# A four-quadrant crossing of query and projection in a window-attention block, and one attention moved at the end

## What is computed

```python
x = x + _conv_bn(x, dw0_w, dw0_s, dw0_b, groups=C)
x = x + _ffn(x, f0_...)
x = x + _windowed_attn(x, wq, wkv, pos, scale_p, dwc_w, dwc_b, proj_w, proj_b)
x = x + _conv_bn(x, dw1_w, dw1_s, dw1_b, groups=C)
x = x + _ffn(x, f1_...)

# _attn, per 7x7 window (the 16x16 image is padded to 21x21, nine windows):
q, kv = xw @ wq.T, xw @ wkv.T              # k gets pos; relu, / softplus(scale)
q, k = _focus(q), _focus(k)                # t**3, norm restored
kv2 = einsum('bjc,bjd->bcd', k, v)         # per head, 4 heads of 16
y = einsum('bic,bcd,bi->bid', q, kv2, z)   # z = 1 / (q . sum k)
y = y + depthwise_5x5(v)
return y @ proj_w.T + proj_b
```

## Time and profile before

| | |
|---|---|
| median of 3 runs | 174.64 us (173.4 to 175.21) |
| the profiled execution | 174.51 us, of which the span from first to last instruction is 172.7 us |
| PE busy | 157.2 us, 91% of the span |
| DVE, ACT, POOL busy | 103.9, 83.7 and 57.5 us (60%, 48%, 33%) |
| mean granted TensorE clock | 0.98 |

### The profile page before, as it was taken

The page is one execution under the profiler, slowest core; times in us unless marked ns, Lnnn a source line. Parts: engine busy times, 40 slices in busy tenths (PEclk is TensorE's granted clock), DMA queues, the critical chain, the costliest instruction groups (busy, mean ns, idle before and its releaser), DMA issues. The chain is left out here.

```text
span 172.7 us, 6668 instructions
## 1 busy us (share of the span) xinstructions
PE 157.2 (91%) x2840; PEld 76.6 (44%) x2840; DVE 103.9 (60%) x270; ACT 83.7 (48%) x178; POOL 57.5 (33%) x75
## 2 busy tenths in 40 slices
PE   6977999899898999999996789999989999987893
PEld 3312252627274873583383562576433425222231
DVE  1168263858777778597588586582189476606043
ACT  2054869494937665756745414653431414033132
POOL 4000028260825504263934926640254312000000
PEclk9999999999999999999999956999999999999999
DMA  5999999940000000000054161063027181959943
GB/s 144 291 245 292 212 215 208 206 84 6 0 4 4 4 4 4 0 4 4 28 141 78 66 143 35 4 171 72 4 76 163 63 173 66 189 167 218 299 140 121
DMA packets 18028, 18.77 MB, mean 109 GB/s; under 512 B 1104, under 2 KB 17744, under 8 KB 17872
## 3 DMA queue, kind: packets, MB, share of 16 engines
q1 hardware_dynamic: 17568, 17.83, 44.6%
q10 hardware_dynamic: 432, 0.52, 1.1%
HBM read 14.16 MB, written 4.19 MB: 106 GB/s over the span
## 5 line engine op out<-in xcount | busy, mean ns | idle before, releaser
L649 PE MATMUL ps<-xc,dwf 96*32 96x480 f32 (+3 forms) x408 | 44.9, 575 | 3.4 <-DMA xc<-mid 2.4
L371 POOL TENSOR_TENSOR qt<-q 128x512 f32<-128x512 f32 x8 | 10.7, 1333 | 57.2 <-ACT q L465 57.2
L649 PEld LDWEIGHTS ps<-xc,dwf 96*32 96x32 f32 x408 | 12.1, 112 | 32.7 <-issue 24.2
L424 ACT ACTIVATE x<-ps,wts 128x512 f32<-128x512 f32 x15 | 10.3, 685 | 26.0 <-PE ps L649 26.0
L671 PE MATMUL ps<-x,w1s 64*128 64x512 f32 x60 | 16.7, 637 | 2.9 <-DVE kvm L1107 1.4
L431 ACT ACTIVATE hid<-ps,wts 128x512 f32<-128x512 f32 x27 | 17.2, 682 | 3.2 <-PE ps L671 3.2
L677 PE MATMUL ps<-hid,w2s 128*64 128x512 f32 x60 | 17.2, 614 | 0.0
L377 POOL TENSOR_TENSOR y<-y,fm 128x512 f32<-128x512 f32 x8 | 10.2, 1274 | 10.7 <-DVE y L1161 7.7
L1061 DVE TENSOR_REDUCE nrm<-k 128x10 f32<-128x640 f32 x8 | 6.6, 819 | 11.6 <-ACT k L459 11.5
L358 POOL TENSOR_TENSOR k<-k 128x640 f32<-128x640 f32 x8 | 12.4, 1550 | 3.4 <-ACT k L453 3.4
L734 PE MATMUL ps<-wts,x 64*64 64x128 f32 x256 | 11.2, 294 | 0.6 <-DVE y L1161 0.6
(11 more groups left out here) (139 smaller groups left out, 277.7 us busy)
## 6 DMA issues: line engine op xcount, KB each, us to landing
xc<-in_x SPq DMA_DIRECT2D x16, 240.0 KB, 11.4
xc<-mid SPq DMA_DIRECT2D x16, 240.0 KB, 4.7
xc<-in_x SPq DMA_DIRECT2D x8, 256.0 KB, 10.7
mid<-x SPq DMA_DIRECT2D x8, 256.0 KB, 2.2
xc<-mid SPq DMA_DIRECT2D x8, 256.0 KB, 3.3
out<-x SPq DMA_DIRECT2D x7, 256.0 KB, 5.7
tab<-in_tables SPq DMA_DIRECT2D x1, 1024.0 KB, 11.4
wts<-in_weights SPq DMA_DIRECT2D x1, 644.0 KB, 7.2
```

The costliest lines, as they stand in the source:

```text
L371: eng.tensor_tensor(qt[:, g % QB, 0:GC], q2[:, g % 2, 0:GC], q1[:, :], ALU.mult).then_inc(qt_ready, 1)
L424: eng.activation(x1[:, m % 2, :], bank(m % 2), ACT.Identity, bias=ww(f"dwb_{m // NG}")).then_inc(x1_ready, 1)
L649: last = eng.matmul(out_ps[32 * q:32 * q + 32, :, :, to], dwf[:, s, q % 2, i, :], src[:, :, :, of], start=(i == 0), stop=False, skip_group ...
```

## The change

Query and projection, which each were two matmuls of 512 columns on the quadrants (0, 0) and (1, 1), become four matmuls of 256 columns on all four quadrants. Image (a, j) of the query goes to column half r = a ^ j and bank `P_B + j`, so q comes out with two of its four images crossed in the partitions; k times v, `window_conv` and the buffers `vfull` and `fm` follow that crossing, and the projection crosses back. With it the banks change: the query fills both banks of `P_B`, the projection of groups 0 to 3 goes to `P_H`, of groups 4 and 5 to a convolution bank and bank 7, of groups 6 and 7 to `P_A`. The waits follow the banks. In slots 6, 7, 9 and 10 `attend` stands ahead of `ffn1`; on DVE `q_first` stands ahead of `k_focus` (slots 5, 6) or ahead of `take_y` (slots 7, 8). At the end `attend(7)` stands directly behind `project(4)`, `conv(11)` behind `project(5)` and `turn_y(6)`, and `project(6)` ahead of `ffn1(11)`; on DVE `take_y(7)` stands ahead of `second(10)`.

```diff
+        def proj_banks(c):
+            if c < 4:
+                return P_H, P_H + 1
+            return (spare(9 + c), P_B + 1) if c < 6 else (P_A, P_A + 1)
...
 def conv(m, n, js=slice(0, GP)):
-                if 0 <= n - 8 < 4:
-                    eng.wait_ge(xw_ready, n - 7)
+                if m in (11, 12):
+                    eng.wait_ge(x3_ready, m - 6)
...
 def ffn1(m, n):
+                if 0 <= n - 7 < 4:
+                    eng.wait_ge(xw_ready, n - 6)
                 if m == 13:
-                    eng.wait_ge(y_ready, NG)
+                    eng.wait_ge(x3_ready, NG)
...
 def query(g, n):
-                for a in range(2):
-                    p = slice(64 * a, 64 * a + 64)
-                    last = eng.matmul(bank(P_B + 1)[p].rearrange("p (j n) -> p j n", j=GP), ww("wq")[p], x2[p, g, :, 0:PX],
-                                      start=True, stop=True)
+                for a, r in QUADRANTS:
+                    j = a ^ r
+                    last = eng.matmul(bank(P_B + j)[64 * r:64 * r + 64, 0:PX], ww("wq")[64 * a:64 * a + 64],
+                                      x2[64 * a:64 * a + 64, g, j, 0:PX], start=True, stop=True)
...
 def kv_rest(g, n):
+                if n == NG:
+                    eng.wait_ge(xw_ready, 2)
...
 def key_value_full(g, n):
-                            last = eng.matmul(bank(P_B + wx)[64 * a:64 * a + 64, VC * s:VC * s + VC], kf[p, g % 2, a, s, :],
-                                              vfull[p, g, 4 * a + s, :], start=True, stop=True)
+                            last = eng.matmul(bank(P_B + wx)[64 * (a ^ j):64 * (a ^ j) + 64, VC * s:VC * s + VC], kf[p, g % 2, a, s, :],
+                                              vfull[p, g // 4, 4 * a + s, g % 4, :], start=True, stop=True)
...
 def turn_y(c, n):
+                if n <= NG:
+                    eng.wait_ge(q_ready, n)
...
 def project(c, n):
                 eng.wait_ge(yt_ready, c + 1)
                 if c < 4:
-                    eng.wait_ge(x2_ready, nextconv(n) - 1)
-                else:
+                    eng.wait_ge(kvr_ready, n - 3)
+                    eng.wait_ge(qn_ready, min(n - 2, NG))
+                    eng.wait_ge(krest_ready, min(n - 1, NG))
+                elif c < 6:
+                    eng.wait_ge(x2_ready, c + 6)
                     eng.wait_ge(kvx_ready, NG)
                     eng.wait_ge(fm_ready, 6)
...
+                else:
+                    eng.wait_ge(y_ready, NG)
+                    if c == 7:
+                        eng.wait_ge(x3_ready, c)
-                for a in range(2):
-                    p = slice(64 * a, 64 * a + 64)
-                    last = eng.matmul(bank(proj_bank(c))[p], ww("proj")[p], yt[p, c % 2, :], start=True, stop=True)
+                for r, a in QUADRANTS:
+                    j, p = r ^ a, slice(64 * r, 64 * r + 64)
+                    last = eng.matmul(bank(proj_banks(c)[j])[64 * a:64 * a + 64, 0:PX], ww("proj")[p],
+                                      yt[p, c % 2, PX * j:PX * j + PX], start=True, stop=True)
...
 window_conv
-                            src = vfull[p, gs, :, NH * dc:NH * dc + NH].rearrange("p g (a j y) h -> p (g a) j y h", a=2, j=2)[:, :, j]
+                            src = vfull[p, half, :, :, NH * dc:NH * dc + NH].rearrange("p (a j y) g h -> p a j (y g) h", a=2, j=2)
+                            src = src[:, ::-1, j] if j else src[:, :, j]
...
 the slots on DVE
+                if n in (7, 8):
+                    q_first(n - 1)
                 take_y(n - 5)
+                if n in (5, 6):
+                    q_first(n - 1)
                 if n - 2 < NG:
                     k_focus(n - 2)
-                if n - 1 < NG:
-                    q_first(n - 1)
```

More of the change, by code:

```diff
@@ L213, in window_block_kernel @@
         kf = sb("kf", 128, 2, 2, 5, C)
-        vfull = sb("vfull", 128, NG, 8, VC)
+        vfull = sb("vfull", 128, 2, 8, 4, VC)
         vrest = sb("vrest", 128, NG, 2, C)
@@ L261, in spare @@
             return nextconv(n) % 2
-        def proj_bank(c):
-            return spare(c + 7) if c < 4 else P_B + 1
+        def proj_banks(c):
+            if c < 4:
+                return P_H, P_H + 1
+            return (spare(9 + c), P_B + 1) if c < 6 else (P_A, P_A + 1)
         def hidden_bank(m):
@@ L435, in take_v_full @@
                 eng.wait_ge(kfull_ready, g + 1)
-                eng.activation(vfull[:, g, :, 0:C], bank(P_A, 2).rearrange("p (s c) -> p s c", c=128)[:, :, C:128], ACT.Copy,
+                eng.activation(vfull[:, g // 4, :, g % 4, 0:C], bank(P_A, 2).rearrange("p (s c) -> p s c", c=128)[:, :, C:128], ACT.Copy,
                                scale=cc("mask0")).then_inc(v_ready, 1)
@@ L526, in take_projected @@
                     eng.wait_ge(x3_ready, c - 1)
-                eng.activation(xw[:, c % 2].rearrange("p j n -> p (j n)"), bank(proj_bank(c)), ACT.Identity,
+                eng.activation(xw[:, c % 2], bank(P_H, 2).rearrange("p (j n) -> p j n", j=GP)[:, :, 0:PX], ACT.Identity,
                                bias=projc[:, 0:1]).then_inc(xw_ready, 1)
@@ L592, in _ @@
                     q_square(n - 1)
+            take_yt(6)
             first(11)
-            take_yt(6)
             hidden(11)
@@ L803, in key_value_rest @@
                     p = slice(64 * j, 64 * j + 64)
-                    last = eng.matmul(bank(P_H + j)[64 * a:64 * a + 64, 0:5 * VC], kf[p, g % 2, a, 4, :],
+                    last = eng.matmul(bank(P_H + j)[64 * (a ^ j):64 * (a ^ j) + 64, 0:5 * VC], kf[p, g % 2, a, 4, :],
                                       vm[p, g % 2, a].rearrange("p w c -> p (w c)"), start=True, stop=True)
@@ L941, in _ @@
                         project(n - 7, n)
+                    attend(n - 5, n)
                     if m is not None:
                         ffn1(m, n)
-                    attend(n - 5, n)
                 if n in FM_SLOT:
@@ L973, in _ @@
             project(4, 11)
+            attend(7, 11)
             ffn1(10, 11)
@@ L976, in _ @@
             ffn2(10)
-            attend(7, 12)
-            conv(11, 12)
             project(5, 12)
             turn_y(6, 12)
+            conv(11, 12)
+            project(6, 13)
             ffn1(11, 12)
-            project(6, 13)
             turn_y(7, 13)
@@ L1048, in q_first @@
                     eng.wait_ge(qt_ready, g)
-                eng.tensor_scalar(q1[:, :], bank(P_B + 1), 0.0, ecol[:, 0:1], ALU.max, ALU.add).then_inc(q_ready, 1)
+                eng.tensor_scalar(q1[:, :].rearrange("p (j n) -> p j n", j=GP), bank(P_B, 2).rearrange("p (j n) -> p j n", j=GP)[:, :, 0:PX],
+                                  0.0, ecol[:, 0:1], ALU.max, ALU.add).then_inc(q_ready, 1)
             def norm2(g):
@@ L1129, in third @@
                 for j in range(GP):
-                    at = PX * j + WIN
+                    src, at = bank(proj_banks(c)[j]), WIN
                     eng.scalar_tensor_tensor(natural(dst, j)[:, :, 14:16], src[:, at:at + 32].rearrange("p (h w) -> p h w", w=2),
@@ L1271, in _ @@
             third(4)
+            take_y(7)
             second(10)
-            take_y(7)
             third(5)
```

19 lines of the change are left out of this document (10 added, 9 removed).

## The result

The changed kernel took 176.56 us (median of 4 runs, 176.06 to 178.67), the kernel before 174.93 beside it (4 runs): ratio 1.0132, 95% interval [1.0076, 1.0188]. On a second chip, with 12 runs, the two could not be told apart: 174.74 against 174.67, 1.001 [0.9971, 1.0048]. Nowhere did it gain the forecast 3.95 us. (Ratios leave disturbed runs out, medians don't; where a median and its ratio disagree, the ratio is meant.)

A forecast was written before the change was run, and what follows sets the result against it. Bounds: TensorE in slots 1 to 5, a ring of engines in slots 6 to 8, transfers at the end. 1.9 - 0.4 + 0.15 + 2.3 = 3.95 us off 174.51 gave 170.6, 8-in-10 range 167.8 to 173.4.

The forecast's parts named there:

- the case that was given 0.70: The main forecast for the whole kernel: 170.6 us, 169.3 to 171.9 with the ends of its terms, chance 0.70.
- Query and projection, 0.45 each: On TensorE, four matmuls of 256 columns on four quadrants take 0.45 us instead of 1.01, saving 0.5 when alone.
- Rival 2: The four quadrants do not overlap, so a query still costs 1.0 us: 175.2 us in all, chance 0.06.
- Slots 1 to 5, 1.9: First five loop passes: each query saves 0.38 us, together 1.9 us (1.2 to 2.8).
- PE time saved there is time saved: Premise for slots 1 to 5: TensorE is nearly always at work, so its savings there shorten the kernel; 1.9 us.
- Slots 6 to 8, -0.4: Middle loop passes: gains of 0.2 and 0.1, loss of 0.7 in slot 8; sum -0.4 us (-1.0 to +0.3).
- the ring: Slots 6 to 8: kv_full, VectorE, ScalarE, GpSimd, ScalarE, then take_y, which releases the next kv_full; q_first on it costs 0.7 us.
- Slots 9 and 10: Slot 9 gains 0.15 us; slot 10 loses 0.6 at ffn2, but attend(6) no longer waits, counted within the end.
- The end, 2.3: Last stretch, slot 10 included: project(5) at 139.0 instead of 141.32, write of group 7 2.3 us earlier.
- Edits at nothing: Layouts, reversed reads, flipped columns, xw, y_sum and third: together 0, bounds -0.2 to +0.4 us of cost.
- Rival 1: Low clock of slots 8 and 9 changes: 167.9 us if its cost comes back (chance 0.09), 177.6 if it lasts (0.05).
- rival 3: At the end, group 5's write meets rows in flight and transfers eat the 2.3 us gain: 172.9 us, chance 0.10.

The follow-up runs named there:

- before_qfirst: The kernel before with one edit of the change alone, q_first ahead of take_y on VectorE in slots 7 and 8: 176.31 us, ratio 1.0045.
- y3: The changed kernel with three buffers of y instead of two, so that take_y(7) waits for turn_y(4): 172.84 us, ratio 0.9892.
- again_after: The changed kernel measured again, unedited: 174.74 us, ratio 1.001 to the kernel before.
- y3_hold168: The changed kernel with three buffers of y and 42 idle one-column matmuls ahead of project(1) in slot 8, a shift of 168 records: 169.87 us, ratio 0.9702.
- after: The changed kernel, unedited, in its first measurement and profile: 176.56 us, ratio 1.0132 to the kernel before.
- before_shift88: The kernel before with three of six warming matmuls replaced by 25 small ones, moving later TensorE instructions by 88 records: 181.58 us, ratio 1.0434.
- after_gaps160: The changed kernel with 40 idle one-column matmuls, 20 behind conv(0) and 20 behind conv(1), a shift of 160 records: 176.07 us, ratio 1.0033.

## Why the prediction was wrong

Forecast 170.6, measured 176.56; the sign was wrong, and neither the case that was given 0.70 nor a rival tells why. Two steps failed, conv(9) in slot 10 and take_y(7) at the end, and one term was mis-sized.

- **Query and projection, 0.45 each: right.** From start to next start 0.48 for the query of slot 1, and 0.44 for the projection of slot 7 (83.03 - 82.59). Rival 2 falls. By the Trainium skill (TensorEngine Tiling (Array Packing), Gotcha 1: PSUM Pressure), different row tiles cannot access one PSUM bank at the same time. Here two row halves write one bank in different partitions, and the four matmuls take 0.48 us, so they overlap.
- **Slots 1 to 5, 1.9: mis-sized, 1.3.** From query to query the slots gained 0.43, 0, 0.26, 0.23 and 0.42. The premise "PE time saved there is time saved" does not hold throughout: in the second stretch ffn1 waits 0.91 us for ScalarE (nrm) instead of 0.50, which swallows all of it, and in the third 0.87 for VectorE (kvm) instead of 0.71.
- **Slots 6 to 8, -0.4: right**, 0.9 - 1.3 = -0.4, and so is its main part: kv_full of slot 8 comes 0.64 later by q_first on the ring (forecast 0.7), shown alone by before_qfirst.
- **Slots 9 and 10: the waits right, the sum wrong.** ffn2 waits for hidden and attend(6) no longer waits, as foreseen. Slot 9 gained 0.9, not 0.15, mostly for another reason: the low clock (100.0 to 106.8 before, 100.6 to 107.4 after) began 1.2 us earlier against kv_full, and conv(8) took 3.98 us instead of 4.55. **The step that failed first** is slot 10 ("Nothing but ffn2 follows ffn1 here"): its sum begins at ffn1 and takes conv(9) over from before, as if PE's time were the sum of its instructions and their waits for other engines. The change adds 88 records ahead of conv(9), which moves a block boundary from key_value_full into conv(9), behind the quickest 256 records of the program. conv(9) took 4.10 us instead of 2.68, and 1.3 to 2.5 longer than 2.68 in the profiles where no low clock follows the stop.
- **The end, 2.3: the step that failed next** is "DVE then does second(10), 0.75, and only then is project(5)'s bank free: 139.0". It left out that take_y(7) stands ahead of second(10) and waits for turn_y(5), which the change itself moves back. project(5) came at 143.00. With a third buffer it comes 10.1 behind attend(6), and from attend(6) to the end y3 takes 41.4 us against 43.4 before: the 2.0 that the forecast had there. The order was right, its buffer was missing.
- **Edits at nothing** show no cost: key_value_full takes 0.70 us and y_sum 1.27 in both kernels. **Rival 1**: the low clock stayed, 6.8 us long, and moved by 1.2 us against kv_full; **rival 3**: the end came late by project(5), not by the rows in flight.
- **The arithmetic afterwards:** the forecast plus 1.9, 172.5, is near the kernel with the third buffer (172.84, 173.64); plus the missed wait of 2 us, 174.5, is near again_after (174.74). Without both, y3_hold168 has 169.87 and 170.21. This proves little: the 1.9 is not conv(9)'s stop alone, and the 0.6 missing in slots 1 to 5 and the 0.75 too much in slot 9 nearly cancel, which is luck. The further 1.8 of the first four runs agrees with the start (24.44 in their profile, 22.8 in that of again_after); that the change has no part in it is not shown.

Left open: why the packet starts late at one boundary and not at another. Counted from the boundary ahead of it, the packet of record 4801 starts 0.71 us later in after, but that of record 705 4.17 in before_shift88 and 8.90 in after_gaps160, there at 33.28, when PE had stood still since 32.27. The packets themselves took 1.3 us there as elsewhere. Inputs are still loading at 220 GB/s then, which may be the reason and was not tried. Open too is how the gain of the shift in slot 8 divides between the stop and the low clock near 100 us.

## What to carry to other kernels

When a step moves up on one engine, list what it moves back there, and ask of each whose buffer it releases: a gain computed with two buffers may need three. On an engine that works through many small instructions, count them: added instructions shift where the fetched blocks end, and a block that arrives later than the engine gets to it shows as a stop that no semaphore explains, at a boundary though not at every one. Such a stop is moved by a few idle instructions put where the engine waits anyway. A control that shifts by a whole block tells it from luck, but read its profile too: the inserted instructions can bring a stop of their own.
